# Graph network, third edge pass: 47 of 1563 gathered tiles fetched row by row by the SP and ACT queues

## The reference, cut to what matters

```python
edge_index = jnp.stack([src, dst])
x = _layernorm(x + _L0_gnn_ref(x, edge_index, 12500, L0_gnn_W))          # softmax over the edges of a node
x = _layernorm(x + _L1_gnn_ref(x, src, dst, ...))                        # attention with 4 heads, then an MLP
x = _layernorm(x + _L2_gnn_ref(x, edge_index, L2_gnn_W, L2_gnn_b))       # graph convolution
x = _layernorm(x + _L3_gnn_ref(x, edge_index, edge_weight, L3_...))      # MLP on every edge, then an update
```

```python
h = x @ W
msgs = h[src] * norm[:, None]                     # norm = dinv[src] * dinv[dst]
out = jax.ops.segment_sum(msgs, dst, num_segments=n) + b
```

## Time and profile before

| what | value |
|---|---|
| timed runs, median of 3 | 10222.5 us (10220.84 to 10224.05) |
| profiled execution, first to last instruction (its span) | 8618.5 us |
| difference of the two | 1604.0 us |
| instructions in the profile | 110748 |
| busy: PE, DVE, ACT, POOL | 4960.4, 5226.5, 2343.8, 6191.1 us |
| third edge pass, first to last gather | 4382.1 to 6332.0 us |
| mean granted TensorE clock | 0.724 of full speed; 0.50 in the third pass |

### The profile page before, as it was taken

How to read it: one execution, slowest core, us unless ns; L and a number is a source line. 1 busy time by engine, 2 the same in 40 slices (tenths; PEclk the granted TensorE clock), 3 DMA queues, 4 the chain that set the end, 5 groups by cost and what they waited for, 6 DMA issues and landing times. The chain is left out here.

```text
span 8618.5 us, 110748 instructions
## 1 busy us (share of the span) xinstructions
PE 4960.4 (58%) x27580; PEld 4002.6 (46%) x27580; DVE 5226.5 (61%) x11719; ACT 2343.8 (27%) x7991; POOL 6191.1 (72%) x6713
## 2 busy tenths in 40 slices
PE   2554445467466666666765544455566666666666
PEld 2443344346355555555543333333355555555553
DVE  6765565567688788878642222222256777777777
ACT  1222222235365656555620000000031111111114
POOL 6777777775777777777257777777767777777775
PEclk9766666668788888888965555555577777777877
DMA  5222222224555555555221111111124444444441
GB/s 129 54 54 54 54 54 54 54 54 141 122 122 123 123 122 123 123 123 122 75 70 53 53 53 53 53 53 53 53 74 130 119 119 119 119 119 119 119 119 41
DMA packets 863047, 769.25 MB, mean 89 GB/s; under 512 B 381750, under 2 KB 720910, under 8 KB 862050
## 3 DMA queue, kind: packets, MB, share of 16 engines
q0 software_dynamic: 231344, 530.57, 23.0%
q1 hardware_dynamic: 622591, 227.53, 10.8%
q10 hardware_dynamic: 8504, 4.07, 0.2%
HBM read 707.23 MB, written 54.29 MB: 88 GB/s over the span
## 5 line engine op out<-in xcount | busy, mean ns | idle before, releaser
L531 POOL DMA_INDIRECT rows_sum<-t_d,idx x1563 | 1474.8, 944 | 688.7 <-issue 476.0
L889 POOL DMA_INDIRECT rows_h<-t_d,idx x1563 | 1482.4, 948 | 521.3 <-issue 459.0
L531 POOL DMA_INDIRECT rows_mlp<-t_d,idx x1563 | 1478.9, 946 | 485.5 <-issue 476.1
L889 POOL DMA_INDIRECT rows<-t_d,idx x1491 | 1409.0, 945 | 464.3 <-issue 444.9
L580 PE MATMUL pn_sum<-S_sum,rows_sum 128*128 128x128 f32 x3126 | 805.0, 439 | 970.2 <-DMA rows_sum<-t_d,idx 961.8
L580 PEld LDWEIGHTS pn_sum<-S_sum,rows_sum 128*128 128x128 f32 x3126 | 692.8, 326 | 1236.1 <-issue 1235.8
L928 ACT ACTIVATE rows_h<-rows_h,wc_h 128x64 f32<-128x64 f32 x4688 | 1134.0, 333 | 9.8
L699 DVE TENSOR_TENSOR big<-big,pn_sum 128x512 f32 x391 | 269.0, 688 | 1430.1 <-PE pn_sum L580 1429.5
L1029 PE MATMUL pn_h<-S_h,rows_h 128*128 128x128 f32 x6252 | 997.4, 314 | 236.4 <-ACT rows_h L928 157.1
L1029 PEld LDWEIGHTS pn_h<-S_h,rows_h 128*128 128x128 f32 x6252 | 921.1, 224 | 383.7 <-issue 351.5
L565 PE MATMUL pre_mlp<-dw_mlp,ST_mlp 128*128 128x128 f32 x3126 | 583.2, 345 | 735.2 <-DVE ST_mlp L55 722.6
(11 more groups left out here) (352 smaller groups left out, 7882.9 us busy)
## 6 DMA issues: line engine op xcount, KB each, us to landing
dw_mlp<-bd_d SPq DMA_DIRECT2D x1563, 64.0 KB
lrb_h<-lrrow_d SPq DMA_DIRECT2D x196, 128.0 KB, 3.1
lrb_mlp<-lrrow_d SPq DMA_DIRECT2D x98, 256.0 KB, 3.5
rows_h<-t_d,idx POOLq DMA_INDIRECT x1563
dw_h<-xp_d SPq DMA_DIRECT2D x1563, 3.0 KB
rows_sum<-t_d,idx POOLq DMA_INDIRECT x1563
rows_mlp<-t_d,idx POOLq DMA_INDIRECT x1563
rows<-t_d,idx POOLq DMA_INDIRECT x1491
```

The costliest lines, as they stand in the source:

```text
L531: e.indirect_dma_start(rows[:, g % NR, j, :], None, table, bass.IndirectOffsetOnAxis(ap=idx[:, b, t:t + 1].bitcast(I32), axis=0)).then_inc ...
L889: e.indirect_dma_start(rows[:, g % NR, j, :], None, table, bass.IndirectOffsetOnAxis(ap=idx[:, b16, t:t + 1].bitcast(I32), axis=0)).then_i ...
```

## The change

Of the 98 blocks, every fourth from block 3 on (24 blocks) gives its last tile to SP, and every fourth from block 5 on (23 blocks) gives its last tile to ACT. In the third pass POOL does not gather these 47 tiles. Each of the two queues fetches its own tiles row by row: for each of a tile's 128 rows one DMA of 512 bytes from the table into one partition of a buffer, with the source's byte offset in a register that was loaded in sixteens. Each queue has three such buffers (DEEP = 3) and reuses one when PE has used the tile in it. PE waits for the tile's own semaphore ahead of its matmul and takes the rows from that buffer.

The byte offsets are made at the start of the pass: DVE multiplies the 47 columns of `idx` by 512, PE transposes them, DVE turns them back into integers, and SP stores them to DRAM and loads them as one list per queue into one partition each. The first, second and fourth pass keep their work; the changes of `landed` and `come` only keep the semaphore counts right.

```diff
+FETCHED = ([NB * b + NB - 1 for b in range(3, 96, 4)], [NB * b + NB - 1 for b in range(5, 96, 4)])
+DEEP = 3
@@ edge_light
+        lanes = ([], []) if mlp else FETCHED
+        lane = {t: (q, k) for q, tiles in enumerate(lanes) for k, t in enumerate(tiles)}
+            frow = [s(f"frow{q}", [P, DEEP, F]) for q in range(2)]
+            fcol, fidx = s("fcol", [P, sum(many)]), s("fidx", [sum(many), P], I32)
+            flist = s("flist", [33, most * P], I32)
+        def near(g):
+            return sum(4 * g + j not in lane for j in range(SIZE[g]))
+
+        def fetch(e, engine, q):
+            byte = table.rearrange("n f -> (n f)").bitcast(U8).rearrange("(o x) -> o x", o=1)
+            for k, t in enumerate(lanes[q]):
+                if k >= DEEP:
+                    e.wait_ge(s_mm, lanes[q][k - DEEP] // 4 + 1)
+                for p in range(0, P, 16):
+                    r0 = load_values(nc, engine, flist[32 * q:32 * q + 1, k * P + p:k * P + p + 16], N * F * 4)
+                    for i in range(16):
+                        e.dma_start(frow[q][p + i:p + i + 1, k % DEEP, :].bitcast(U8), byte[:, bass.ds(r0[i], F * 4)]
+                                    ).then_inc(s_far[q][k % DEEP], 16)
@@ SP, behind the weight loads
+                e.wait_ge(s_fx, 3)
+                e.dma_start(d["far"], fidx[:, :]).then_inc(s_dd, 16)
+                e.wait_ge(s_dd, 16)
+                for q in range(2):
+                    if many[q]:
+                        e.dma_start(flist[...], d["far"][...]).then_inc(s_dd, 16)
+                listed = 16 + 16 * sum(n > 0 for n in many)
+                e.wait_ge(s_dd, listed)
                 e.wait_ge(s_pv, 3)
                 e.dma_start(d["deg"], deg[:, :, :]).then_inc(s_dd, 16)
-                e.wait_ge(s_dd, 16)
+                fetch(e, SP, 0)
+                e.wait_ge(s_dd, listed + 16)
@@ POOL
+                    if 4 * g + j in lane:
+                        continue
@@ ACT
+        if not mlp and many[1]:
+            @block.scalar
+            def _(e):
+                e.wait_ge(s_dd, 48)
+                fetch(e, mybir.EngineType.Activation, 1)
@@ PE
+                e.wait_ge(s_fx, 1)
+                e.transpose(px[0:sum(many), :], fcol[:, :], c["ident"][:, :]).then_inc(s_fx, 1)
@@ PE, place
-                    last = e.matmul(pn[g % 2][:, bass.ds(r0[j], P)], rows[:, g % NR, j, :], S[:, g % NS, j, :],
+                    x = rows[:, g % NR, j, :]
+                    if 4 * g + j in lane:
+                        n, k = lane[4 * g + j]
+                        e.wait_ge(s_far[n][k % DEEP], before[n][k % DEEP] + 16 * P * (k // DEEP + 1))
+                        x = frow[n][:, k % DEEP, :]
+                    last = e.matmul(pn[g % 2][:, bass.ds(r0[j], P)], x, S[:, g % NS, j, :],
@@ DVE
+                for q in range(2 if many[1] else 1):
+                    f0, f1 = q * many[0], q * many[0] + many[q]
+                    b0 = lanes[q][0] // NB
+                    e.tensor_scalar(fcol[:, f0:f1], idx[:, b0:b0 + 4 * many[q] - 3:4, NB - 1].bitcast(I32), float(F * 4), None, ALU.mult)
+                e.drain().then_inc(s_fx, 1)
+                e.wait_ge(s_fx, 2)
+                e.tensor_copy(fidx[:, :], px[0:sum(many), :])
+                e.drain().then_inc(s_fx, 1)
```

More of the change, by code:

```diff
@@ L78, in prog @@
     deg_d = dram("deg_d", (NT, 3, P), BF16)
+    far_d = dram("far_d", (sum(map(len, FETCHED)), P), I32)
     lrn_d = dram("lrn_d", (NT, P), BF16)
@@ L106, in prog @@
         d = dict(pen=pen_d, rowpen=rowpen_d, lrrow=lrrow_d, wcol=wcol_d, x=t0_d[:, 0:F],
-                 deg=deg_d, lrn=lrn_d, t1=t1_d, t2=t2_d, t3=t3_d, xp=xp_d, bd=bd_d)
+                 deg=deg_d, lrn=lrn_d, far=far_d, t1=t1_d, t2=t2_d, t3=t3_d, xp=xp_d, bd=bd_d)
         with ExitStack() as ctx:
@@ L477, in edge_light @@
             s_w, s_dd, s_p, s_pv = sem("s_w"), sem("s_dd"), sem("s_p"), sem("s_pv")
+            most = max(map(len, lanes))
+            many = [len(tiles) for tiles in lanes]
+            frow = [s(f"frow{q}", [P, DEEP, F]) for q in range(2)]
+            fcol, fidx = s("fcol", [P, sum(many)]), s("fidx", [sum(many), P], I32)
+            flist = s("flist", [33, most * P], I32)
+            px = ps("px", [P, P])
+            s_fx = sem("s_fx")
+            s_far = [c["s_in"], [sem(f"s_far{i}") for i in range(DEEP if lanes[1] else 0)]]
+            before = [list(c["come"]), [0] * DEEP]
         s_g, landed = c["s_g"], list(c["landed"])
@@ L480, in edge_light @@
         block = ctx.enter_context(nc.Block(no_gpsimd_drain=True))
+        def near(g):
[10 more added lines that the diff above has]
+                                    ).then_inc(s_far[q][k % DEEP], 16)
         def gathered(g):
-            return s_g[g % NR], landed[g % NR] + 16 * sum(SIZE[k] for k in range(g % NR, g + 1, NR))
+            return s_g[g % NR], landed[g % NR] + 16 * sum(near(k) for k in range(g % NR, g + 1, NR))
         def windows(g):
@@ L504, in _ @@
                     e.dma_start(t[:, :], row(n, k)).then_inc(s_w, 16)
+                e.wait_ge(s_fx, 3)
[3 more added lines that the diff above has]
+                    if many[q]:
+                        e.dma_start(flist[32 * q:32 * q + 1, 0:many[q] * P],
+                                    d["far"][q * many[0]:q * many[0] + many[q], :].rearrange("t e -> (t e)").rearrange("(o x) -> o x", o=1)
+                                    ).then_inc(s_dd, 16)
+                listed = 16 + 16 * sum(n > 0 for n in many)
+                e.wait_ge(s_dd, listed)
                 e.wait_ge(s_pv, 3)
                 e.dma_start(d["deg"], deg[:, :, :]).then_inc(s_dd, 16)
-                e.wait_ge(s_dd, 16)
+                fetch(e, SP, 0)
+                e.wait_ge(s_dd, listed + 16)
                 return
@@ L720, in _ @@
             e.drain()
+    for k in range(0 if mlp else len(FETCHED[0])):
+        c["come"][k % DEEP] += 16 * P
     for g in range(GR):
-        c["landed"][g % NR] += 16 * SIZE[g]
+        c["landed"][g % NR] += 16 * (SIZE[g] if mlp else sum(4 * g + j not in FETCHED[0] + FETCHED[1] for j in range(SIZE[g])))
 CHAIN = ("score", "scoreT", "scan1", "row1", "scanI", "col1", "scan2", "row2", "scanJ", "col2", "scan3", "exp",
```

## The result

The changed kernel took **10660.92 us** (median of 4 runs, 10655.49 to 10676.72) against 10221.67 us (4 runs, 10218.63 to 10224.05) for the kernel before beside it: ratio 1.0423, 95% interval 1.0403 to 1.0443, 439 us slower. Forecast were 10164 us and a gain of 58.7.

What follows compares the result with a forecast made beforehand. POOL's gather issuing was taken to bound the third pass: 47 skipped gathers save 58.7 us, the other terms add 0, so 10222.5 - 58.7 = 10163.8, say 10164 us; range 10146 to 10202.

Steps and rivals of the forecast that it cites:

- the profile shows nothing of that part. I take it as unchanged: Timed runs lie 1604.0 us above the profile's span; this part was taken as unchanged, giving 10163.8 us.
- the same work at a slower pace: Alternative for the 1604 us: whole kernel slower by 1.186, so the gain is 69.6 us and the time 10152.9.
- What bounds the kernel: Third pass: POOL's issuing is the whole bound, number of gathers x 1.2483 us plus two ends; PE waits for rows.
- What goes: Third pass: POOL skips 47 of 1563 gathers at 1.2483 us each, saving 58.7 us.
- The price of a row: Fetching one row costs 0.474 us on SP, 0.531 on ACT, under the 0.605 budget, so the lanes add 0.
- The start: Start of third pass: making the offsets is hidden; SP's lane begins near 4397, its first tile ready at 4460, wanted 4462.
- POOL beside the lanes: Third pass: the lanes' DMAs slow POOL's gathers by 0 to +16 us; taken as 0.
- Rival 1: Third pass: a row on SP or ACT costs over 0.605 us, so a lane sets the pass; +142 to +516 us; chance 0.10.
- Rival 2: The 1604 us outside the span grow with the added instructions: net +121 to +208 us; chance 0.06.
- Rival 3: Third pass: POOL or its transfers slow beside the lanes and pay back part of the gain: 10184 to 10222; chance 0.08.
- The chances: Whole kernel: faster 0.79, same 0.05, slower 0.16; the forecast itself had 0.76.

Runs made afterwards that it cites:

- e4: The changed kernel with its 47 fetched tiles, unchanged, run again beside the kernel before: 8569.74 us against 8620.03, ratio 0.9944.
- e14: The kernel before without the 47 gathers of the third pass and nothing in their place: 8572.35 us against 8627.85, ratio 0.9933.
- e7: The changed kernel with a fetched tile in every third block per queue, 31 + 31 tiles: 8551.56 us against 8620.03 for the kernel before, ratio 0.9920.
- e10: The kernel before, unchanged, profiled again for its trace: 10277.49 us.
- e11: The changed kernel with a fetched tile in every eighth block per queue, 12 + 12 tiles: 10287.4 us, ratio 1.0027 to the kernel before.
- e16: Same kernel as e14, the kernel before without the 47 gathers, run again: 8576.1 us against 8634.83, ratio 0.9931.
- e17: Same kernel as e14 and e16, the kernel before without the 47 gathers, run again: 8565.86 us against 8623.09, ratio 0.9933.
- e3: The changed kernel, but POOL gathers all 1563 tiles and the lanes also fetch the 47 into buffers PE does not read: 8641.9 us, ratio 1.0008.
- e15: Same kernel as e3, all 1563 gathers plus 47 tiles fetched but not read, run again: 8631.78 us against 8627.85, ratio 1.0007.
- e13: The kernel before plus 16 semaphore waits per group on SP and ACT in the third pass, moving no data: 10328.43 us, ratio 1.0070.
- e8: The changed kernel, 47 tiles, with row offsets loaded two at a time and not sixteen: 11366.12 us against 10232.92 for the kernel before, ratio 1.1112.

## Why the prediction was wrong

- **The step that failed** is "the profile shows nothing of that part. I take it as unchanged". The 1604 us are not outside the span. They are spread through it: span and time differ by 1.8 us in every execution whose own time is known. The alternative I named ("the same work at a slower pace") was nearer and still wrong, because POOL's pace is the same; the 1604 us are stops. Every duration of the working came from an execution of a kind that the timed runs did not have, and the term that turned the sign is the lanes', put at 0: 0.474 us a row under a budget of 0.605 forecast, 0.858 measured. The mark was in the first table: a time 19% above the span of the profile.
- **What bounds the kernel** holds in the short kind (e4, e14, e7) and fails in the long one. There POOL stands 291.7 us of e10's third pass with a full ring, PE's wait for gathered rows is no longer among the waits, and e11 skips 24 gathers and the kernel is 27 us slower and not 30 faster.
- **What goes**: -58.7 forecast; -57.8 for the pass and -50.3 for the kernel in e4, -55 to -59 for the gathers alone (e14, e16, e17). Right there, and absent from the timed result.
- **The price of a row**: 0.474 us on SP and 0.531 on ACT forecast, 0.40 on both measured in the short kind (0.42 where the lanes never waited, e3 and e15). Its terms erred both ways: there is no address instruction, the DMA takes 228 and 218 ns and not 248 and 329, but the load of 16 values takes 1.23 and 1.30 us and not 0.685 and 0.307. In the long kind it was 0.858 on SP, above the budget of 0.605 and above the 0.69 that the long kind's own pass leaves, and the sign was decided there.
- **The start** held: e4's lane begins at 4399.5 (forecast 4397), and PE reached its first fetched tile at 4468.8 without waiting. **POOL beside the lanes** held: 0 forecast, +0.07% to +0.08% with zero in the interval (e3, e15).
- **Rival 1** (0.10) is what happened: 24 waits of PE on fetched rows, POOL behind PE, a loss inside the band of 142 to 516 us that I gave it. The cause I gave for it was not seen: two queues at 0.40 us a row each ran side by side in e4. It was the pace of the queues in the long kind, where one lane alone was not run. Its own sum for a dear row ((0.858 - 0.605) x 2900 = 734 us) is above the measured 407, because the pass of the long kind is 277 us longer to begin with and the budget there 88/128 = 0.69 us a row: (0.858 - 0.69) x 2900 = 487. The rest of the difference was not looked into.
- **Rival 2** (0.06), a part outside the span that grows with the instructions, did not occur: that part is 1.8 us in both kernels. What grows with them is the backlog of a queue inside the span (e13).
- **Rival 3**, POOL slower beside the lanes, did not occur: 0.947 us for a gather in both kernels of the long kind, 0.945 in both of the short one, and e3 and e15 above.
- **The chances**: the slower side had 0.16. It hung on the same unread mark; with a time 1604 us above the span, no price of that profile deserved 0.76.

The Trainium skill's rule that issuing from several engines saves a time "usually small relative to the DMA itself" ("DMA: Bandwidth & Descriptors", "Issuing engines are not separate DMA queues") does not decide here in the short kind, where 0.56% to 0.80% was gained because the pass consists of that issuing.

**Open.** Why PE's reports come late and single queue instructions take 0.7 us was not found, nor what puts an execution in one kind or the other. The record has one strong hint. It numbers the chip of each experiment: all 39 executions on chip 15 (e8 to e13 and the kernel before beside them) were long, and all 111 on chips 5, 7, 8, 10 and 11 were short. So the kind went with the chip and not with the kernel; the chips of the first runs are not on record, no chip showed both kinds, and no run tells what is different about it. Nor does any run tell whether recording an execution has a part in it. Whether leaving out the 47 gathers gains anything in the long kind was not measured. Why e11's pass is longer with 24 gathers fewer is not shown either: its one late tile accounts for 26 us of POOL's waits, and a single profile of each stands against the other.

## What to carry to other kernels

Compare the span of a profile with the timed runs before reading a single duration from it; where they lie far apart, the profile is of another kind of execution, and its bound and its prices may not be those of the time that counts. A lane that is issued one small DMA at a time must be priced by the pace of its queue beside working engines, not by the median of its instructions, and with slack: here 0.40 us a row became 0.86, and 1.23 where the lane held nobody up, against a budget of 0.605. Measure both kernels on more than one chip before believing a gain or a loss of a few per cent. The pace of an idle queue can be measured alone, as e13 does: add instructions without the data, and see how far they fall behind.

## What the runs showed of the hardware

- A DMA of 512 B to one partition with its source offset in a register takes one MOVE of 29 ns and 228 ns on SP or 218 on ACT, and 0.32 and 0.31 us from one to the next (e4, medians); the load of 16 register values takes 1.23 and 1.30 us.
- Such a row is not spread over the DMA engines: in e4 every row adds two packets to its queue, one of 512 B and one of 4 B (ACT's queue: 8504 packets before, 14392 with 2944 rows). Which engine took it is not shown.
- Two queues at 0.40 us a row each did not disturb each other, nor a GpSimd that issues a 128-row gather every 1.25 us.
- In the long kind SP's queue took 0.54 us per wait instruction beside the working engines and 0.063 us once they had ended (e13).
- The same kernel ran in 8625 us and in 10277 us with the same busy time of POOL (6197.1 and 6204.8 us) and gathers of 0.945 and 0.947 us. In the long kind register moves of 29 ns take up to 1422, PE's finished group reaches DVE 6.3 us after its last matmul and not 0.15 (medians), and the mean granted TensorE clock is 0.683 against 0.726, with PE idle longer.
